# Grouped attention with 64-wide heads: pairing heads of two key groups, and turning row maxima and multiplying sums in two batches

## What is computed

```python
def _L2_attn_ref(X, Wq, Wk, Wv, Wpost):
    # NUM_HEADS 16, NUM_GROUPS 4, HEADS_PER_GROUP 4, KEY_WIDTH = VALUE_WIDTH = 64
    Q = (X @ Wq).reshape(n, s, NUM_GROUPS, HEADS_PER_GROUP, KEY_WIDTH)
    K = (X @ Wk).reshape(n, s, NUM_GROUPS, KEY_WIDTH)
    V = (X @ Wv).reshape(n, s, NUM_GROUPS, VALUE_WIDTH)
    raw = jnp.einsum('bsgwe,btge->bstgw', Q, K * scale)
    attn = jax.nn.softmax(raw, axis=2)
    A = jnp.einsum('bstgw,btge->bsgwe', attn, V).reshape(n, s, NUM_HEADS * VALUE_WIDTH)
    return X + A @ Wpost

x = x + _layernorm(_L2_attn_ref(_layernorm(x, axis=-1), L2_attn_Wq, L2_attn_Wk, L2_attn_Wv, L2_attn_Wpost), axis=-1)
```

## Time and profile before

| | |
|---|---|
| median of 3 runs | 1063.32 us (1063.27 to 1073.59) |
| profiled execution, span | 1093.7 us |
| TensorE busy | 946.4 us, 87% |
| VectorE busy | 730.1 us, 67% |
| ScalarE busy | 561.5 us, 51% |
| GpSimd busy | 472.5 us, 43% |
| stage of the change in the profile | about 575 to 845 us |

### The profile page before, as it was taken

One profiled execution on the slowest core, in us unless ns is written; L12 is line 12 of the kernel. 1 busy time (PEld: TensorE's weight loads), 2 busy tenths in 40 slices (PEclk: granted clock), 3 DMA queues, 4 the chain that ended last, 5 costly groups with the idle time before them and its releaser, 6 DMA issues. The chain is left out here.

```text
span 1093.7 us, 24314 instructions
## 1 busy us (share of the span) xinstructions
PE 946.4 (87%) x8249; PEld 744.2 (68%) x8264; DVE 730.1 (67%) x2020; ACT 561.5 (51%) x1164; POOL 472.5 (43%) x528
## 2 busy tenths in 40 slices
PE   6999987867999399999879999999999967768990
PEld 5666666767998376666566667777666856768990
DVE  4677654545666577887577566766676778755664
ACT  2667762223665247787545554544545435225662
POOL 2355664444344522322364333343456432774443
PEclk9999997889999599999999999999999979988995
DMA  9221110021121312422120011101111720022214
GB/s 304 64 63 54 54 56 1 27 58 38 44 58 31 77 41 61 133 62 79 43 60 21 2 41 41 42 13 29 41 41 41 281 54 1 30 67 58 57 45 116
DMA packets 80754, 66.46 MB, mean 61 GB/s; under 512 B 6706, under 2 KB 73441, under 8 KB 80251
## 3 DMA queue, kind: packets, MB, share of 16 engines
q1 hardware_dynamic: 71899, 54.34, 17.6%
q0 software_dynamic: 4512, 8.47, 2.3%
q10 hardware_dynamic: 4224, 2.10, 0.8%
HBM read 38.76 MB, written 26.58 MB: 60 GB/s over the span
## 5 line engine op out<-in xcount | busy, mean ns | idle before, releaser
L822 DVE TENSOR_REDUCE a_rowmax<-a_banks 128x4 f32<-128x1024 f32 (+1 forms) x112 | 136.8, 1222 | 50.3 <-PE a_banks L1205 19.6
L2771 POOL TENSOR_TENSOR a_both<-a_probs 128x512 f32<-128x512 f32 x64 | 86.4, 1350 | 142.5 <-ACT a_probs L3080 142.4
L1024 ACT ACTIVATE a_probs<-a_banks 128x1024 f32<-128x1024 f32 x112 | 114.9, 1026 | 56.4 <-PE a_banks L1191 44.5
L1800 POOL DMA_INDIRECT acc<-m_result,m_yb x77 | 75.5, 980 | 105.7 <-DVE m_result L2119 58.9
L3080 ACT ACTIVATE a_probs<-a_banks 128x1024 f32<-128x1024 f32 x64 | 65.6, 1025 | 85.5 <-PE a_banks L3253 85.5
L1793 POOL DMA_INDIRECT rows<-m_yrow,m_idx x64 | 64.1, 1001 | 57.2 <-issue 22.6
L2929 DVE TENSOR_REDUCE a_rowmax<-a_banks 128x4 f32<-128x1024 f32 x64 | 77.7, 1219 | 13.1 <-PE a_banks L3226 13.1
L2262 ACT ACTIVATE m_gate<-m_banks 128x352 f32<-128x352 f32 (+1 forms) x93 | 42.9, 462 | 77.2 <-PE m_banks L2471 60.7
L3269 PE MATMUL a_banks<-a_probs,a_V 128*64 128x256 f32 x512 | 69.4, 392 | 0.0
L2497 PE MATMUL m_banks<-e_down,m_hT_hi 128*128 (+2 forms) x231 | 65.2, 350 | 0.6 <-DVE m_hT_lo L2102 0.6
L691 POOL TENSOR_SCALAR_AFFINE_SELECT a_probs<-a_probs 128x512 f32<-128x512 f32 (+1 forms) x48 | 37.9, 790 | 63.8 <-ACT a_probs L1024 63.7
(11 more groups left out here) (418 smaller groups left out, 2778.4 us busy)
## 6 DMA issues: line engine op xcount, KB each, us to landing
rows<-fill SPq DMA_DIRECT2D x16, 520.0 KB, 4.3
a_factor<-recip_rows SPq DMA_DIRECT2D x28, 256.0 KB, 4.6
rows<-fill SPq DMA_DIRECT2D x15, 455.0 KB, 4.0
m_yb<-rows SPq DMA_DIRECT2D x77, 65.0 KB
a_expert<-in_experts SPq DMA_DIRECT2D x16, 257.5 KB
e_gu_lo<-in_gu SPq DMA_DIRECT2D x1, 2736.0 KB
e_last_row<-in_last_rows SPq DMA_DIRECT2D x1, 2736.0 KB
e_gu_lo<-in_gu SPq DMA_DIRECT2D x1, 2464.0 KB, 12.3
```

The source lines that it names most:

```text
L822: nc.vector.reduce_max(o, src, AX).then_inc(rowmax_ready, 1)
L1024: nc.scalar.activation(probs[h][:, k, :, :], ps[:, 4:6, :], ACT.Exp, scale=SCALE).then_inc(exp_done, 1)
L1800: nc.gpsimd.indirect_dma_start(acc.rearrange("k n d -> (k n) d"), bass.IndirectOffsetOnAxis(yb[b % YB][:, P:P + 1].bitcast(U32), 0), resul ...
L2771: nc.gpsimd.tensor_tensor(both[u % 4][:, :, :], p[:, :, 0, :], p[:, :, 1, :], ALU.add).then_inc(both_ready, 1)
```

## The change

Pair u now holds one head of each of two key groups: groups 2m and 2m + 1, with m = u // 4. The queries' weights and the output weights are reordered to that on the host (`head_of`), and each group's keys are projected once, into one half of the partitions. `K` is [128, 2, 256], and `project_k` is one call of two blocks. The low part, the rounded copy and the raw copy of keys are halved in the same way.

Row maxima are turned in two batches of four pairs (in step 4, and in step 0 of the next slot), copied by two ScalarE instructions of 8 partitions, and placed by two pairs of DMAs. Sums are multiplied in two batches of four pairs, at the same two steps. `both` has eight buffers instead of four, so the exponentials wait for GpSimd's add and no longer for the sums.

```diff
+def head_of(pair, h):
+
+    return HG * (2 * (pair // HG) + h) + pair % HG
...
-                K[part][k] = over.sb(f"k_{part}{k}", [P, NG, SEQ], F32R)
+                K[part][k] = over.sb(f"k_{part}{k}", [P, NG // 2, SEQ], F32R)
...
+        both = [over.sb(f"both{k}", [P, 2, SEQ]) for k in range(S)]
...
-            def place(i, j):
-                sp.wait_ge(mrow_ready, NG * i + j + 1)
+            def place(i, b):
+                sp.wait_ge(mrow_ready, 2 * i + b + 1)
...
                 if s - 3 in valid:
-                    place(s - 3, NG - 1)
+                    place(s - 3, 1)
                 if s - 4 in valid and s - 4 != LAST:
                     spread(s - 4)
                 if s - 2 in valid:
-                    for j in range(NG - 1):
-                        place(s - 2, j)
+                    place(s - 2, 0)
...
                 if u == 4 and ip in valid:
                     low_q(ip, 3)
-                    low_k(ip, 0)
-                if u == 5 and ip in valid:
-                    low_k(ip, 1)
+                    low_k(ip)
...
-                    row(i2, 3)
-                if u in (3, 5, 7) and i1 in valid:
-                    row(i1, (u - 3) // 2)
+                    row(i2, 1)
+                if u == 5 and i1 in valid:
+                    row(i1, 0)
...
-                    act.wait_ge(sums_ps, n // 2 + 1)
+                    act.wait_ge(both_ready, n + 1)
...
-                if n == 0:
-                    pe.wait_ge(mrow_placed[j], 32 * (i + 1))
+                if u % HG == 0:
+                    pe.wait_ge(mrow_placed[u // HG], 32 * (i + 1))
...
-                pe.wait_ge(both_ready, S * i + 2 * j + 2)
-                for h in range(2):
-                    for n in range(2):
-                        k = 2 * n + h
-                        last = mm(ps[k * COLS:(k + 1) * COLS, 7, 0:SEQ], sum_cols[:, j, :], both[(2 * j + n) % 4][:, h, :],
-                                  start=j == 0, stop=j == NG - 1)
+                pe.wait_ge(both_ready, S * i + HG * (b + 1))
+                for j in (2 * b, 2 * b + 1):
+                    for h in range(2):
+                        for n in range(2):
+                            k = 2 * n + h
+                            last = mm(ps[k * COLS:(k + 1) * COLS, 7, 0:SEQ], sum_cols[:, j, :], both[2 * j + n][:, h, :],
+                                      start=j == 0, stop=j == NG - 1)
...
-                    if v % 2 == 1:
-                        sums(i, v // 2)
+                    if v % HG == HG - 1:
+                        sums(i, v // HG)
...
-                if u in (2, 4, 6) and i1 in valid:
-                    if NG * i1 + u // 2 - 1:
-                        pe.wait_ge(mrow_ready, NG * i1 + u // 2 - 1)
-                    if u == 2 and ip in valid:
-                        pe.wait_ge(q_lo, NG * ip + 1)
-                    if u == 4 and ip in valid:
+                if u == 4 and i1 in valid:
+                    if i1:
+                        pe.wait_ge(mrow_ready, 2 * i1)
+                    if ip in valid:
                         pe.wait_ge(q_lo, NG * ip + 4)
-                    if u == 6 and ip in valid:
-                        pe.wait_ge(v_ready, ip + 1)
-                    row_maxima(i1, u // 2 - 1)
+                    row_maxima(i1, 0)
...
-                    project_k(ip, 0)
-                if u == 4 and ip in valid:
-                    if ip >= 1:
-                        pe.wait_ge(k_lo, 2 * ip + 1)
-                    project_k(ip, 1)
+                    project_k(ip)
```

More of the change, by code:

```diff
@@ L2628, in grouped_attention_ffn @@
         probs = [st.sb(f"probs{k}", [P, 2, T, SEQ]) for k in range(4)]
-        both = [st.sb(f"both{k}", [P, 2, SEQ]) for k in range(4)]
         recip = st.sb("recip", [P, SEQ])
@@ L2665, in first_raw @@
         def first_raw(part, n):
-            k = n if part == "q" else NG + n
+            k = n if part == "q" else NG
             return probs[1 + k // 2][:, k % 2, :, :]
@@ L3116, in prologue @@
                 high_q(1, 3)
-                row(0, 2)
             def finished(s, u):
@@ L3300, in project_q, with project_k @@
                 last.then_inc(q_ps, 1)
-            def project_k(i, n):
-                for h in range(2):
-                    o = 2 * n + h
-                    last = mm(ps[:, bank_k(i, n), h * SEQ:(h + 1) * SEQ], at["wk"][:, o * P:(o + 1) * P], yT[:, :],
+            def project_k(i):
+                for m in range(NG // 2):
+                    last = mm(ps[:, bank_k(i), m * SEQ:(m + 1) * SEQ], at["wk"][:, m * P:(m + 1) * P], yT[:, :],
                               start=True, stop=True)
```

169 lines of the change are left out of this document (75 added, 94 removed).

## The result

The changed kernel takes 1054.24 us (median of 4 runs, 1051.25 to 1067.33) beside 1064.68 (1063.27 to 1073.59) of the kernel before: 0.989 times the time, interval 0.9855 to 0.9928. The ratio leaves out an execution of the changed kernel that ran in a slower state (1067.33), which the median counts. The forecast was 1054.7 with a range of 1049.5 to 1060.0, and "within 1%". Measured twice more, on two chips, the change gave 0.9928 (0.9896 to 0.9960) and 0.9942 (0.9912 to 0.9973), so a gain of 0.6 to 1.1%, or 6 to 12 us; in the mean of the three 0.80%, which is 8.5 us of 1064.68. The first ratio lies just past the forecast's 1%, the other two within it.

A forecast was written before the change was run, and what follows sets the result against it. TensorE at full clock bounds the attention stage; -11.8 +2.7 +0.9 in the slots, -1.3 at the start and +0.9 at the end total -8.6 us, from the median 1063.32 to 1054.7 us, range 1049.5 to 1060.0.

The forecast's parts named there:

- Bound by TensorE: Inner slots (eight steps each) of the 64-wide attention: TensorE work removed shortens the slot until another engine is late.
- Steps 2, 4, 6 and 0: Inner slot, by TensorE work: step 2 -0.69 us, step 4 -0.41, step 6 -0.87 if nobody is late, step 0 +0.45.
- The upper bound: Sums batch of four pairs in step 4 or 0: 1.14 us if the second call costs in full; forecast 1.4 us higher.
- Slots 3 to 8: Full slots of the attention stage: steps 2, 4, 6 give -11.8 us, step 0 +2.7, VectorE's lateness +0.9.
- VectorE late in step 6: Step 6 of slots 4 to 8: row maxima end after TensorE is ready, +0.15 to 0.2 us each, +0.9 in all.
- Start, -1.3: Before the first full slot: two key projections dropped, gaining 0.4 and 0.96 us; bounds 0 and -2.5.
- End, +0.9: Slots 9, 10 and last sums: -0.1 us, +0.45 and +0.1, +0.45; later steps wait for the factors' DMA and exponentials.
- The rival of GpSimd and VectorE in each other's way: Inner step 6: multiplication takes 1.23 us, not 0.68, so step 7 starts 0.55 later; total -5.8, 1057.5 us; chance 0.11.
- A granted clock below 1.00 in the stage: TensorE's clock in the 64-wide attention stage: assumed full; a lower one was listed as making the forecast wrong.
- Nothing late: Whole stage: VectorE early enough, end gains like inner slots, start gains 2.5; -12.9 us, 1050.4; chance 0.22 with lucky later stages.
- late rows: Step 0 scores wait for placed row maxima past 8.3 us after their copy; 1075 us or more; chance 0.04.
- no gain: Whole stage: TensorE's saved time all comes back as waits, 1063 us; chance 0.03.

The follow-up runs named there:

- keys projected twice: The changed kernel with each key projection issued twice into the same bank; 0.9979 of the time of the kernel before (0.9945 to 1.0013).
- batches only: The kernel before with only the two batches of row maxima and sums, old head pairing and key projections kept; 0.9966 of its time (0.9937 to 0.9994).
- the one made warm: The changed kernel plus five identity matmuls in TensorE's idle gaps at the stage's start; 0.9951 of the time of the kernel before (0.9917 to 0.9984).
- keys only: The kernel before with only the new head pairing and single key projection, maxima and sums in four batches; 0.9942 of its time (0.9916 to 0.9968).
- the changed kernel's second profile: The changed kernel run again without edit; 0.9928 of the time of the kernel before (0.9896 to 0.9960), stage 270.44 us.

## Why the prediction was right, and where not

The time and the sign were right: -8.6 us forecast, 8.5 in the mean of three timings. That 1054.24 lies within half a microsecond of 1054.7 is partly luck: the kernel before took 1064.68 in that comparison and not the 1063.32 that the sum started from, so the two medians lie 10.4 us apart. Of its terms some were exact, and three were off with signs that partly cancel.

- **Bound by TensorE.** Shown, by keys projected twice: in step 3 of the inner slots +0.87 of work is +0.87 of step.
- **Steps 2, 4, 6 and 0.** Step 2 -0.69 forecast and -0.67 to -0.69 measured; step 4 -0.41 and -0.44; step 6 -0.87 + 0.18 and -0.67; step 0 +0.45 and +0.43. The batch was taken as 1.02 from half of a projection's spacing and is 1.00. The upper bound, two calls in full (1.14), is refuted; that goes with the rule on changes of tiling mode that the prediction weighed (the Trainium skill, TensorEngine Tiling (Array Packing), Key Properties), and is no proof of it, since batches only shows the same 1.00 and no run puts one change more into the queue. Slots 3 to 8: -8.2 forecast, -8.46 in the one profile whose clock did not fall, and -8.45 in the one made warm.
- **VectorE late in step 6.** Right in place, size and cause: 0.2 us a slot, which goes when the multiplication stands behind the maxima.
- **Start, -1.3.** The step that failed is the 0.4 for the first key projection: the start gained 0.9. The second projection's 0.96 is there. The first gave nothing: with keys only TensorE waits 1.18 us for row maxima instead, and the start gains 0.85. The turn's later wait (0.56 for the row copy, in the fence on the start) was named but not charged; batches only, where it stands alone, costs 0.28.
- **End, +0.9.** Three pieces behaved differently. The +0.45 behind the last sums came as forecast: 11.82 became 12.25. In slot 9 "0.1 earlier" was 0.17 where the DMA landed late, and 1.01 where it landed early. In slot 10, where +0.45 and +0.1 were charged, it was +1.5, -0.1 and +1.1. The sum of the end was +1.8, -0.7 and +0.6 in three profiles of one kernel. The step that failed is "its steps 1 to 7 again hang on the factors' DMA": it priced the landing as a fixed time and did not ask what is queued on VectorE behind the multiplication (the moments, hence L384, hence L499), nor how near the landing lay to GpSimd's add. In the kernel before the landing of 11.38 was just in front of the edge, which lies between 11.38 and 11.40.
- **The rival of GpSimd and VectorE in each other's way.** Refuted where it was put: the multiplication in inner step 6 stayed at 0.68. The same mechanism was real at the end, where nobody had put it. The Trainium skill, SBUF — State Buffer, Who interferes with whom, says that a tensor_tensor with both inputs in SBUF contends with GpSimd's reads, and that the order of issue decides which of the two blocks; 0.69 against 1.23 to 1.65, and 1.29 against 2.38 for two, agree, and so do the starts in slot 10.
- **A granted clock below 1.00 in the stage.** The prediction named it as what would make it wrong, and looked only at an inner slot and the end in the profile of before. It came where the start meets slot 3, in 7 of 8 profiles of kernels with single key projections and none of the added work, and in none of the six others: +1.54 us, not in the sum. The first profile of the change happened to be the one without it. The prediction also passed over the stretch ahead of the first maxima scores, which runs partly at the lower clock in every profile.
- **Nothing late** is refuted by step 6 and the end, **late rows** by the absence of any wait for placed rows in the inner slots, **no gain** by the ratios.

Term by term for the changed kernel's second profile: +0.3 ahead of the first maxima scores, -0.9 start, -8.4 slots without the clock, +1.5 clock, -0.7 end, together -8.1. In the first: +0.4 -0.9 -8.5 +1.8, together -7.2. The forecast of 8.6 hit 8.5 as timed with a stage that gained 7.0 to 8.1, 7.4 in the mean, so part of that hit is luck; the half to one and a half microseconds between are within the timings' spread, and no run explains them.

## What to carry to other kernels

Where one engine fills its slots, the starts of its groups give a change to a few hundredths of a microsecond a step; put the doubt, and the range, on the edges, where engines wait. For each small DMA that an in-order engine waits for, ask what stands behind the waiting instruction and how far the landing is from the next one that shares a port: work that depends on nothing late goes ahead of it. When a change takes work off TensorE near a place where it already stands idle a few times, look at the granted clock just behind that place, and try a few dummy matmuls in the gaps.

## What the runs showed of the hardware

- The clock of TensorE fell to its lower level for part of one step behind three idle gaps of under 0.8 us each, in kernels that project keys once: 5.86 against 4.31 us for one step. With five small matmuls in the gaps it stayed at 1.00, and so it did behind the same gaps in two kernels with more projections. It depended on the execution too: one profile of eight went without the fall.
- A context multiplication on VectorE is 0.69 us alone and 1.23 to 1.65 when it meets GpSimd's add; two of them 1.29 and 2.38. A landing 0.07 us later (11.33, 11.40) was the difference.
- From a reciprocal to the multiplication by its factors, two small DMAs and their waits, 11.2 to 12.3 us, and up to 0.7 us apart between executions of one kernel.
- Eight more records in a batch of sums cost 0.43 us where the call already stands, less than the 0.57 us of a call of its own.
- An expert layer that no kernel here changes took 173.2 to 173.6 us on one chip and 194.7 to 196.8 on two others, while steps of the attention stage agree within 0.02 us across chips.
